# Masked attention scores: row maxima split into three bf16 parts on GpSimd, causal masks only on the diagonal blocks

## The chip, the core and the metric

The kernel runs on one core of one Trainium2 chip. Five engines work side by side, each through its own queue in program order: TensorE (PE, with its weight loads PEld), VectorE (DVE), ScalarE (ACT), GpSimd (POOL) and SyncE (SP, which issues most DMAs). They wait for each other by semaphores. The metric is device time in microseconds: the kernel before took 677.0 us, the median of three runs (675.83 to 677.92).

## The reference, cut to what matters

Two layers, each with a recurrence ("condition"), a causal attention over 4 batches of 256 tokens with 16 heads of 16 dimensions, a second condition and a feed-forward part (a quantised linear layer in the first, a mixture of 32 experts in the second). The change lies in the two attentions:

```
q, k, v = proj(Wq, bq), proj(Wk, bk), proj(Wv, bv)           # 16 heads of 16
scores = einsum('bhsd,bhtd->bhst', q, k) / sqrt(16)
scores = where(t > s, -inf, scores)                          # causal
attn = softmax(scores, axis=-1)
out = einsum('bhst,bhtd->bhsd', attn, v);  y = out @ Wo.T + bo
```

## The kernel before, in words

All engines' programs are written by hand in one function, `build`; the order on an engine is the order of the code, and waits stand where the code has `wait_ge`. Each attention goes through 16 quads v of four heads (batch b = v // 4, place u = v % 4). Four heads of 16 dimensions sit in slots of 32 partitions, so four products with 32 rows each can stand on PE at once. The PSUM tile S holds one bank per head, with 384 columns: query tile 0 against key tile 0, and query tile 1 against both key tiles. The scores of a quad are made twice:

- `scores` (L688, L692): queries on partitions. It starts with a product of the identity and a mask of 384 columns per head and adds q times k. `maxima` (L1095, DVE) reduces them along the keys and writes the negated maxima into `negmax`, one column in 32.
- `neg_mm` (L720): PE turns `negmax` in fp32 by a product with the identity; `neg_out` (L452, ACT) copies the turned rows to SBUF as `neg_rows`.
- `turned_scores` (L702, L706, L710): keys on partitions. A mask again, then k times q, and `pick` (a row of ones per slot) times `neg_rows`, which adds each query's negated maximum to its column. It waits for the maximum of the quad after, since both forms use S.
- `exps` (L445, ACT) takes the exponential of S; `pv` (L739) multiplies by the values and sums the rows.

On PE a step of the loop is: the scores of quad v + 1, `pv` of v - 1, the turned scores of v, `neg_mm` of v + 1, then one of the projections in 11 of 16 steps per layer: queries or keys (L638), values (L664) or the output (L676). The turning of v + 1 thus stands in front of the projection and of the scores of v + 2, which also wait for the exponential of v. On DVE the maximum of v + 1 is followed by a share of the recurrence of another batch: in even steps two small tensor_scalar pieces (L958), a forward and a backward scan (L967, L979) and the scaling of the attention output; in odd steps the two scans of the other half and five products (L998 to L1017 or L1033). In the last step of batches 1 to 3 the residual of the batch before (L1115) comes first. In layer 1 the last two steps have no recurrence.

POOL does little before the experts: fills with zeros and ones, a maximum over partitions of the weight (L342) before the first maximum, one of the activations (L346) between the layers, four additions (L350) before the second attention, and from 389.93 us on the scattering of rows.

Of the kernel before, what the change touches and what calls it, by code (L numbers as in the profile page):

```python
# [13 lines left out]
P = 128  # L14
# [14 lines left out]
SLOT = 32  # L29
# [29 lines left out]
def build(nc, A, out):  # L59
    ctx = ExitStack()  # L60
    with ctx:
        def sb(name, shape, dt=F32):
            return ctx.enter_context(nc.sbuf_tensor(name, shape, dt))
# [31 lines left out]
        causal_b = sb("causal_b", [P, 2, 3 * P], BF16)  # L95
# [15 lines left out]
        negmax = sb("negmax", [P, 2, T // P, HPT, SLOT])  # L111
        neg_rows = sb("neg_rows", [P, 2, T])
        pick = sb("pick", [P, P])
# [210 lines left out]
        def _(eng):  # L324
            eng.memset(v_sb[:, :, :, :, :], 0.0).then_inc(sem("v_zeroed"), 1)
            eng.memset(negmax[:, :, :, :, :], 0.0).then_inc(sem("negmax_zeroed"), 1)
# [4 lines left out]
            for i in range(HPT):  # L331
                eng.memset(pick[i * SLOT:i * SLOT + 1, :], 1.0).then_inc(sem("pick_made"), 1)
            eng.wait_ge(sem("pick_made"), 1 + HPT)
            for par in range(2):
# [5 lines left out]

            eng.wait_ge(sem("amax_w"), 1)
            eng.partition_all_reduce(gmax[:, 1:2], amax_w[:, :], P, bass.bass_isa.ReduceOp.max)\  # L342
               .then_inc(sem("gmax_w"), 1)

# [3 lines left out]
            for b in range(B):  # L348
                eng.wait_ge(sem("y8_made"), b + 1)
                eng.tensor_tensor(x[:, :, tok(b)], x[:, :, tok(b)], y8[:, :, tok(b)], ALU.add).then_inc(sem("x_res_8"), 1)  # L350

# [36 lines left out]
        def _(eng):  # L388
# [58 lines left out]
            def neg_out(L, v):  # L447

                eng.wait_ge(sem(f"neg_mm_{L}"), v + 1)
                if v >= 2:  # L450
                    eng.wait_ge(sem(f"turned_score_{L}"), v - 1)
                eng.activation(neg_rows[:, v % 2, :], TB[:, 0, 0:T], ACT.Copy).then_inc(sem(f"neg_out_{L}"), 1)  # L452
# [180 lines left out]
        def _(eng):  # L633
# [45 lines left out]

            def scores(L, v):  # L680

                b, u = v // QUADS, v % QUADS
                if u == 0:
                    eng.wait_ge(sem(f"k_out_{L}"), b + 1)
                if v >= 2:
                    eng.wait_ge(sem(f"exp_{L}"), v - 1)
                for i in range(HPT):
                    eng.matmul(S[:, i, 0:3 * P], ident_b[:, :], causal_b[:, 0, :], start=True, stop=False)  # L688
                for st, cols in HALVES:
                    for i in range(HPT):  # L690
                        rows = slice(i * SLOT, (i + 1) * SLOT)
                        ins = eng.matmul(S[:, i, cols], q_sb[rows, b % 2, u, st * P:(st + 1) * P],  # L692
                                         k_sb[rows, b % 2, u // 2, 0:P * (st + 1)], start=False, stop=st == 1)
                ins.then_inc(sem(f"score_{L}"), 1)

            def turned_scores(L, v):

                b, u = v // QUADS, v % QUADS
                eng.wait_ge(sem(f"max_{L}"), min(v + 2, B * QUADS))
                eng.wait_ge(sem(f"neg_out_{L}"), v + 1)  # L700
                for i in range(HPT):
                    eng.matmul(S[:, i, 0:3 * P], ident_b[:, :], causal_b[:, 1, :], start=True, stop=False)  # L702
                for kt, (q_cols, cols) in enumerate(((slice(0, T), slice(0, T)), (slice(P, T), slice(T, 3 * P)))):
                    for i in range(HPT):
                        rows = slice(i * SLOT, (i + 1) * SLOT)
                        eng.matmul(S[:, i, cols], k_sb[rows, b % 2, u // 2, kt * P:(kt + 1) * P],  # L706
                                   q_sb[rows, b % 2, u, q_cols], start=False, stop=False)
# [4 lines left out]
                ins.then_inc(sem(f"turned_score_{L}"), 1)  # L712
# [216 lines left out]
        def _(eng):  # L929
# [158 lines left out]
            def maxima(L, v):  # L1088

                eng.wait_ge(sem(f"score_{L}"), v + 1)  # L1090
                eng.wait_ge(sem("negmax_zeroed"), 1)
                if v >= 2:
                    eng.wait_ge(sem(f"neg_mm_{L}"), v - 1)
                for st, cols in HALVES:
                    ins = eng.tensor_reduce(negmax[:, v % 2, st, :, 0], S[:, :, cols], AX.X, ALU.max, negate=True)  # L1095
                ins.then_inc(sem(f"max_{L}"), 1)
# [267 lines left out]
def layout(inputs):  # L1364
# [23 lines left out]
    a["causal"] = np.stack([np.concatenate([m, np.zeros((P, P)), m], 1) for m in (causal, causal.T)], 1).astype(bf16)  # L1388
# [40 lines left out]
```

## Time and profile before

| | |
|---|---|
| three runs | 675.83, 677.92, 677.0 us |
| the profiled execution | 678.75 us, its span 676.9 us |
| mean granted PE clock | 0.925 |
| busy: PE, DVE, ACT, POOL | 523.4, 432.0, 275.4, 211.8 us |
| first and last maximum, layer 0 | 42.19 and 168.54 us |
| first and last maximum, layer 1 | 219.54 and 341.48 us |

Busy time is a sum over stages with different limits, so the attentions have to be read by themselves. A row of the timeline has the start, the busy time and the engine, the line and what is written from what; where an engine stood idle before it, the end of the row says for how long and who ended the wait. A granted clock of 1.00 is the 2.4 GHz level of PE, 0.50 the 1.2 GHz level.

### The profile page before, as it was taken

The numbers are of one execution on the slowest core, as the hardware profiler recorded it, in microseconds if no ns is written. First come the engines' busy times: TensorE is split into PE (matmuls) and PEld (weight loads), VectorE is DVE, ScalarE is ACT, GpSimd is POOL, SyncE is SP. The second block draws the span as 40 slices with busy tenths as digits, with TensorE's granted clock in tenths as the row PEclk, the third lists the DMA queues.
The fourth block names the chain that finished last, engine by engine and source line by source line (L and its number), as shares of the span: only waits on it lengthen the run. The fifth ranks groups of instructions, "written<-read, shape, count | busy, mean of one in ns | idle before, by whom it ended". The sixth has DMA issues, their size and how long they took to land.

```text
span 676.9 us, 12242 instructions
## 1 busy us (share of the span) xinstructions
PE 523.4 (77%) x4564; PEld 407.6 (60%) x4564; DVE 432.0 (64%) x834; ACT 275.4 (41%) x557; POOL 211.8 (31%) x169
## 2 busy tenths in 40 slices
PE   0278799998716779999875689169999999999950
PEld 0156566665404456666654355059999999999940
DVE  3748699999882779999936833036566566566510
ACT  3323464654533445454534111024444444444420
POOL 2000000000012000000000577705778777687772
PEclk9999799999966999999996599679999999999995
DMA  7999910000000000000003233275997869769423
GB/s 279 267 219 223 227 47 1 2 2 1 1 1 0 1 2 1 2 1 2 2 1 135 91 116 110 98 225 143 220 216 197 221 163 228 210 174 225 108 23 68
DMA packets 56716, 71.97 MB, mean 106 GB/s; under 512 B 11777, under 2 KB 45036, under 8 KB 56544
## 3 DMA queue, kind: packets, MB, share of 16 engines
q1 hardware_dynamic: 40272, 57.48, 30.2%
q0 software_dynamic: 16400, 13.87, 11.1%
q8 instruction: 30, 0.49, 0.3%
q14 instruction: 14, 0.11, 0.1%
HBM read 42.22 MB, written 37.04 MB: 117 GB/s over the span
## 4 chain that ended last, share of the span: by engine, by line
PE 49%; DVE 26%; issue 9%; POOL 7%; ACT 5%; DMA 2%; POOLq 0%; SPq 0%; DVEq 0%
PE S L894 14%; DVE negmax L1095 8%; PE PJ L907 8%; POOL xe_rows L358 6%; PE OB L907 4%; PE TB L879 3%; PE S L692 3%; PE S L706 2%; DVE both L979 2%; PE PJ L676 2%; PE S L702 2%; PE PJ L638 2%; DVE fwd L967 2%; PE S L688 2%; PE S L710 2%
## 5 line engine op out<-in xcount | busy, mean ns | idle before, releaser
L894 PE MATMUL S<-xgT,wgu_s 128*128 128x384 f32 x576 | 108.6, 341 | 1.2 <-DVE hidden_f L1336 1.2
L358 POOL DMA_INDIRECT xe_rows<-x_tok,slot_i x48 | 47.2, 984 | 182.5 <-ACT x_tok L577 168.1
L894 PEld LDWEIGHTS S<-xgT,wgu_s 128*128 128x128 f32 x576 | 99.3, 189 | 1.5 <-issue 1.4
L369 POOL DMA_INDIRECT out<-sig,y_token x48 | 75.9, 1581 | 46.6 <-ACT sig L612 33.9
L1095 DVE TENSOR_REDUCE negmax<-S 128x4 f32<-128x512 f32 x64 | 58.3, 952 | 46.0 <-PE S L692 34.1
L369 POOL DMA_INDIRECT odd_out<-sig,y_token x48 | 76.6, 1595 | 24.4 <-ACT sig L612 12.3
L445 ACT ACTIVATE prob<-S 128x1536 f32<-128x1536 f32 x32 | 46.4, 1449 | 66.1 <-PE S L710 66.1
L907 PE MATMUL PJ<-x8m,hidden_f 128*128 128x256 f32 x256 | 60.5, 379 | 1.4 <-ACT sig L612 1.4
L1333 DVE TENSOR_TENSOR hidden_f<-ek,S 128x384 f32<-128x384 f32 x32 | 17.7, 554 | 56.9 <-ACT ek L595 56.9
L907 PEld LDWEIGHTS PJ<-x8m,hidden_f 128*128 128x128 f32 x256 | 47.9, 190 | 6.7 <-issue 1.8
L346 POOL PARTITION_ALL_REDUCE amax_x<-amax_x x1 | 0.4, 380 | 162.2 <-DVE amax_x L1085 162.2
L1325 DVE TENSOR_TENSOR xgT<-TB,xgT 128x384 fp32r<-128x384 f32 x64 | 32.9, 552 | 25.6 <-ACT xgT L602 25.5
L612 ACT ACTIVATE sig<-PJ,y_weight 128x256 f32<-128x256 f32 x64 | 26.8, 471 | 54.1 <-PE OB L907 52.4
L879 PE MATMUL TB<-ident,ratio 128*128 128x128 f32 x192 | 27.6, 282 | 20.2 <-DMA ratio<-xe_rows 19.6
L702 PE MATMUL S<-causal_b,ident_b 128*128 128x384 bf16 x128 | 26.5, 330 | 19.3 <-DVE negmax L1095 19.3
L638 PE MATMUL PJ<-cst,wq 128*128 128x256 f32 x64 | 18.6, 442 | 28.5 <-DVE cst L1033 28.5
L979 DVE TENSOR_TENSOR_SCAN both<-decay_t,fwd 128x512 f32<-128x512 f32 x32 | 39.2, 1225 | 1.1
L595 ACT ACTIVATE ek<-S 128x384 f32<-128x384 f32 x32 | 15.7, 490 | 59.4 <-PE S L894 59.4
L688 PE MATMUL S<-causal_b,ident_b 128*128 128x384 bf16 x128 | 27.4, 339 | 15.3 <-ACT k_sb L489 8.4
L967 DVE TENSOR_TENSOR_SCAN fwd<-decay_t,ek 128x512 f32<-128x512 f32 x32 | 38.9, 1214 | 0.0
L879 PEld LDWEIGHTS TB<-ident,ratio 128*128 128x128 f32 x192 | 23.8, 146 | 24.0 <-DMA ratio<-xe_rows 20.0
L602 ACT ACTIVATE xgT<-TB 128x384 fp32r<-128x384 f32 x64 | 28.4, 504 | 21.5 <-PE TB L879 21.1
(178 smaller groups left out, 1018.0 us busy)
## 6 DMA issues: line engine op xcount, KB each, us to landing
xe_rows<-x8m SPq DMA_DIRECT2D x4, 3468.0 KB, 41.9
ratio<-xe_rows SPq DMA_DIRECT2D x32, 433.5 KB, 4.1
ek<-in_wgu SPq DMA_DIRECT2D x32, 384.0 KB, 4.6
x8m<-in_wd SPq DMA_DIRECT2D x32, 256.0 KB, 2.9
x<-in_x SPq DMA_DIRECT2D x1, 1024.0 KB, 7.3
odd_out<-x8m SPq DMA_DIRECT2D x1, 1024.0 KB, 29.3
out<-side SPq DMA_DIRECT2D x8, 128.0 KB, 5.5
out<-odd_out POOLq DMA_DIRECT2D x1, 1024.0 KB, 7.9
```

The costliest lines, as they stand in the source:

```text
L358: eng.indirect_dma_start(xe_rows, bass.IndirectOffsetOnAxis(slot_i[:, t, k:k + 1], 0), x_tok[:, t, :], None, bounds_check=ROWS - 1, oob_is ...
L369: eng.indirect_dma_start((out, odd_out)[j % 2], bass.IndirectOffsetOnAxis(y_token[:, j, t:t + 1], 0), ye_sb[:, j % 2, t, :], None, bounds_ ...
L445: eng.activation(prob[:, v % 2, :, :], S[:, :, 0:3 * P], ACT.Exp).then_inc(sem(f"exp_{L}"), 1)
L688: eng.matmul(S[:, i, 0:3 * P], ident_b[:, :], causal_b[:, 0, :], start=True, stop=False)
L702: eng.matmul(S[:, i, 0:3 * P], ident_b[:, :], causal_b[:, 1, :], start=True, stop=False)
L879: ins = eng.transpose(TB[:, k, t * P:(t + 1) * P], xg[:, j % RINGE, t, k * P:(k + 1) * P], ident[:, :])
L894: ins = eng.matmul(S[:, m, 0:CAP], fast(wgu_s[:, j % 2, a, k, m * P:(m + 1) * P]), fast(xgT[:, j % 2, b, k, :]), start=n == 0, stop=n == N ...
L907: ins = eng.matmul(dst, hidden_f[:, j % 2, part, t * P:(t + 1) * P], wd[:, j % RINGE, part, :], start=part == 0, stop=part == 1)
L967: eng.tensor_tensor_scan(flat(fwd[:, kv, :, :]), decay_t[:, buf, 0:NC * T], ek_of(kv, b), 0.0, ALU.mult, ALU.add).then_inc(sem("forward"), 1)
L979: eng.tensor_tensor_scan(flat(both[:, kv, :, :])[:, ::-1], decay_t[:, buf, NC * T:0:-1], flat(fwd[:, kv, :, :])[:, ::-1], 0.0, ALU.mult, A ...
L1095: ins = eng.tensor_reduce(negmax[:, v % 2, st, :, 0], S[:, :, cols], AX.X, ALU.max, negate=True)
L1325: eng.tensor_tensor(fast(xgT[:, j % 2, LO, k, :]), TB[:, k, 0:CAP], xgT[:, j % 2, HI, k, :], ALU.subtract)\
```

## The change

POOL splits the fp32 negated maxima of a quad into three bf16 parts (a copy to bf16, the rest, its copy, the rest of that), in four instructions of 128 x 8 elements that each wait for the one before. PE turns the three parts as bf16 columns, three products of 128 columns (query tile 1 stands twice, so that one product per head of 384 columns can add them), and `pick` has three rows of ones per slot. Masks are products of 128 columns, only for the two diagonal blocks of a head, and stand behind the scores. The maxima now wait for POOL's split of two quads ago and no longer for the turning.

```diff
+            def split_maxima(L, v):
+                at = 4 * (B * QUADS * L + v)
+                eng.wait_ge(sem(f"max_{L}"), v + 1)
+                if v >= 2:
+                    eng.wait_ge(sem(f"neg_mm_{L}"), v - 1)
+                settle(eng, "pool")
+                eng.tensor_copy(neg_parts[:, v % 2, :, :, 0], negmax[:, v % 2, :, :]).then_inc(sem("split"), 1)
+                eng.wait_ge(sem("split"), at + 1)
+                eng.tensor_tensor(neg_rest[:, :, :], negmax[:, v % 2, :, :], neg_parts[:, v % 2, :, :, 0], ALU.subtract)\
+                   .then_inc(sem("split"), 1)
+                eng.wait_ge(sem("split"), at + 2)
+                eng.tensor_copy(neg_parts[:, v % 2, :, :, 1], neg_rest[:, :, :]).then_inc(sem("split"), 1)
+                eng.wait_ge(sem("split"), at + 3)
+                eng.tensor_tensor(neg_parts[:, v % 2, :, :, 2], neg_rest[:, :, :], neg_parts[:, v % 2, :, :, 1], ALU.subtract)\
+                   .then_inc(sem("split"), 1)
...
+            def mask_diagonals(turned):
+                for i in range(HPT):
+                    for lo in (0, 2 * P):
+                        ins = eng.matmul(S[:, i, lo:lo + P], ident_b[:, :], causal_b[:, turned, :], start=False,
+                                         stop=lo > 0, skip_group_check=True)
+                return ins
...
-                for i in range(HPT):
-                    eng.matmul(S[:, i, 0:3 * P], ident_b[:, :], causal_b[:, 0, :], start=True, stop=False)
                 for st, cols in HALVES:
...
+                mask_diagonals(0).then_inc(sem(f"score_{L}"), 1)
...
-                    eng.matmul(S[:, i, 0:3 * P], ident_b[:, :], causal_b[:, 1, :], start=True, stop=False)
+                    rows = slice(i * SLOT, (i + 1) * SLOT)
+                    eng.matmul(S[:, i, 0:3 * P], pick[rows, :], neg_rows[rows, v % 2, :], start=True, stop=False,
+                               skip_group_check=True)
...
-                    for i in range(HPT):
-                        rows = slice(i * SLOT, (i + 1) * SLOT)
-                        ins = eng.matmul(S[:, i, cols], pick[rows, :], neg_rows[rows, v % 2, q_cols], start=False,
-                                         stop=kt == 1)
...
+                mask_diagonals(1).then_inc(sem(f"turned_score_{L}"), 1)
...
-                eng.wait_ge(sem(f"max_{L}"), v + 1)
+                eng.wait_ge(sem("split"), 4 * (B * QUADS * L + v + 1))
...
-                for st in range(T // P):
-                    ins = eng.matmul(TB[:, 0, st * P:(st + 1) * P], negmax[:, v % 2, st, :, :].rearrange("p i s -> p (i s)"),
-                                     ident[:, :], start=True, stop=True)
+                for n, st in enumerate((0, 1, 1)):
+                    ins = eng.matmul(TB[:, 0, n * P:(n + 1) * P], neg_parts[:, v % 2, st, :, :].rearrange("p i s -> p (i s)"),
+                                     ident_b[:, :], start=True, stop=True)
```

On PE, the second turned scores of layer 0 and the turning behind them, in the order of the kernel before:

```order
L702 MATMUL S<-causal_b,ident_b 128x384 [waits neg_out_0,max_0]
L702 MATMUL S<-causal_b,ident_b 128x384 x3
L706 MATMUL S<-q_sb,k_sb 128x256 x4
L710 MATMUL S<-neg_rows,pick 128x256 x4
L706 MATMUL S<-q_sb,k_sb 128x128 x4
L710 MATMUL S<-neg_rows,pick 128x128 x4
L720 MATMUL TB<-ident,negmax 128x128 [waits neg_out_0,max_0]
L720 MATMUL TB<-ident,negmax 128x128
```

The same place on PE in the changed kernel, whose line numbers are about 30 higher:

```order
L738 MATMUL S<-neg_rows,pick 128x384 [waits neg_out_0,max_0]
L738 MATMUL S<-neg_rows,pick 128x384 x3
L743 MATMUL S<-q_sb,k_sb 128x256 x4
L743 MATMUL S<-q_sb,k_sb 128x128 x4
L712 MATMUL S<-causal_b,ident_b 128x128 x8
L753 MATMUL TB<-ident_b,neg_parts 128x128 [waits neg_out_0,split]
L753 MATMUL TB<-ident_b,neg_parts 128x128 x2
```

Eight products of picked maxima became four, the masks moved from the front to the back and from four to eight, and the turning waits for `split` in place of the maximum.

```order
L342 ISA
L342 ISA gmax<-amax_w 128x1 [waits amax_w]
L346 ISA amax_x<-amax_x 128x4 [waits amax_x]
L350 ISA
L350 TENSOR_TENSOR x<-x,y 128x2x256 [waits y8_made] x4
```

The same place on POOL in the changed kernel, to the end of the second split:

```order
L362 ISA
L362 ISA gmax<-amax_w 128x1 [waits amax_w]
L351 CAST neg_parts<-negmax 128x8 [waits neg_parts_zeroed,max_0]
L353 ISA
L353 TENSOR_TENSOR neg_rest<-negmax,neg_parts 128x8 [waits split]
L356 CAST neg_parts<-neg_rest 128x8 [waits split]
L358 TENSOR_TENSOR neg_parts<-neg_rest,neg_parts 128x8 [waits split]
L351 CAST neg_parts<-negmax 128x8 [waits max_0]
```

## Rows read from the trace of the kernel before

**Rows 1.** The page's slices of the span, the granted clock of TensorE

```profile
PEclk9999799999966999999996599679999999999995
```

**Rows 2.** Windows of single quads: length, busy time by engine (instructions), granted clock, DMA

```profile
128.47:136.65 8.18, 7.67 (x104) 5.37 (x103) 7.60 (x11) 5.65 (x11) 0.00 (x0) 1.00 0.01 2
136.65:144.83 8.18, 7.67 (x104) 5.37 (x103) 7.24 (x14) 4.61 (x10) 0.00 (x0) 1.00 0.01 2
144.83:153.30 8.47, 7.96 (x108) 5.52 (x107) 8.30 (x12) 3.74 (x7) 0.00 (x0) 1.00 0.01 2
160.85:168.54 7.69, 6.25 (x100) 3.98 (x99) 7.52 (x10) 3.66 (x6) 0.00 (x0) 1.00 0.01 2
```

**Rows 3.** Timeline of one quad with a projection, and what DVE starts in others

```profile
130.21 1.22 DVE L967 TENSOR_TENSOR_SCAN fwd<-decay_t,ek 128x512 f32<-128x512 f32 x1
130.35 0.82 PE L702 MATMUL S<-causal_b,ident_b 128*128 128x384 bf16 x4 [0.51 <-DVE negmax L1095]
131.10 0.71 PE L706 MATMUL S<-q_sb,k_sb 32*128 32x256 f32 x8
131.64 0.61 PE L710 MATMUL S<-neg_rows,pick 32*128 32x256 f32 x8
131.66 1.23 DVE L979 TENSOR_TENSOR_SCAN both<-decay_t,fwd 128x512 f32<-128x512 f32 x1
132.62 0.71 PE L720 MATMUL TB<-ident,negmax 128*128 128x128 f32 x4
132.76 1.45 ACT L445 ACTIVATE prob<-S 128x1536 f32<-128x1536 f32 x1 [1.91 <-PE S L710]
133.17 1.89 PE L638 MATMUL PJ<-cst,wk 128*128 128x256 f32 x8
...
134.90 0.81 PE L688 MATMUL S<-causal_b,ident_b 128*128 128x384 bf16 x4
136.65 1.82 DVE L1095 TENSOR_REDUCE negmax<-S 128x4 f32<-128x512 f32 x2 [0.41 <-PE S L692]
138.39 0.60 DVE L958 TENSOR_SCALAR eu<-side,vec 128x256 f32<-128x256 f32 x2
...
146.57 0.87 DVE L1115 SCALAR_TENSOR_TENSOR x<-PJ,vec,x 128x256 f32<-128x256 f32 x2
```

**Rows 4.** Groups of 90 to 170 us: weight loads of the masks, count, busy, mean ns

```profile
L688 PEld LDWEIGHTS S<-causal_b,ident_b 128*128 128x128 bf16 x40 | 3.7, 98 | 4.7 <-ACT prob L445 2.2
```

**Rows 5.** Timeline of POOL at the start, a fill of one element per partition

```profile
5.60 0.11 POOL L338 MEMSET inner<- 128x1 f32 x1
```

**Rows 6.** Timeline between the two attentions: POOL's additions, DVE and ACT beside them

```profile
198.73 0.69 ACT L561 ACTIVATE y<-S,scale_ab 128x512 bf16<-128x512 f32 x1 [1.86 <-PE S L785]
201.16 2.71 POOL L350 TENSOR_TENSOR x<-x,y 128x512 f32<-128x512 f32 x2 [7.46 <-issue]
204.64 0.69 DVE L1127 TENSOR_TENSOR c_all<-c_all,x8m 128x512 f32<-128x512 f32 x1
204.74 1.61 POOL L350 TENSOR_TENSOR x<-x,y 128x512 f32<-128x512 f32 x1 [0.88 <-ACT y L561]
205.37 1.53 DVE L1129 TENSOR_TENSOR x<-c_all,x8m 128x512 bf16<-128x512 f32 x1
208.78 1.15 POOL L350 TENSOR_TENSOR x<-x,y 128x512 f32<-128x512 f32 x1 [2.44 <-ACT y L561]
```

**Rows 7.** Timeline of the first maxima and scores of layer 0, and of two later ones

```profile
42.19 1.82 DVE L1095 TENSOR_REDUCE negmax<-S 128x4 f32<-128x512 f32 x2 [11.62 <-issue]
44.88 0.81 PE L688 MATMUL S<-causal_b,ident_b 128*128 128x384 bf16 x4
47.09 1.81 DVE L1095 TENSOR_REDUCE negmax<-S 128x4 f32<-128x512 f32 x2
...
74.75 1.46 PE L688 MATMUL S<-causal_b,ident_b 128*128 128x384 bf16 x4 [3.40 <-ACT k_sb L489]
77.87 1.82 DVE L1095 TENSOR_REDUCE negmax<-S 128x4 f32<-128x512 f32 x2 [5.23 <-PE S L692]
```

More of the change, by code:

```diff
@@ L94, in build @@
         ident_b = sb("ident_b", [P, P], BF16)
-        causal_b = sb("causal_b", [P, 2, 3 * P], BF16)
+        causal_b = sb("causal_b", [P, 2, P], BF16)
         decay_qg = sb("decay_qg", [P, CONDS * NC, B])
@@ L110, in build @@
         bq_masked = sb("bq_masked", [P, NC, 2])
-        negmax = sb("negmax", [P, 2, T // P, HPT, SLOT])
-        neg_rows = sb("neg_rows", [P, 2, T])
-        pick = sb("pick", [P, P])
+        negmax = sb("negmax", [P, 2, T // P, HPT])
+        neg_rest = sb("neg_rest", [P, T // P, HPT])
+        neg_parts = sb("neg_parts", [P, 2, T // P, HPT, SLOT], BF16)
+        neg_rows = sb("neg_rows", [P, 2, 3 * P], BF16)
+        pick = sb("pick", [P, P], BF16)
         ones_p = sb("ones_p", [P, 2, SLOT])
@@ L325, in _ @@
             eng.memset(v_sb[:, :, :, :, :], 0.0).then_inc(sem("v_zeroed"), 1)
-            eng.memset(negmax[:, :, :, :, :], 0.0).then_inc(sem("negmax_zeroed"), 1)
+            eng.memset(neg_parts[:, :, :, :, :], 0.0).then_inc(sem("neg_parts_zeroed"), 1)
             eng.memset(pick[:, :], 0.0).then_inc(sem("pick_made"), 1)
@@ L331, in _ @@
             for i in range(HPT):
-                eng.memset(pick[i * SLOT:i * SLOT + 1, :], 1.0).then_inc(sem("pick_made"), 1)
+                eng.memset(pick[i * SLOT:i * SLOT + 3, :], 1.0).then_inc(sem("pick_made"), 1)
             eng.wait_ge(sem("pick_made"), 1 + HPT)
@@ L343, in _ @@
                .then_inc(sem("gmax_w"), 1)
+            eng.wait_ge(sem("neg_parts_zeroed"), 1)
+            for v in range(B * QUADS):
+                split_maxima(0, v)
             eng.wait_ge(sem("amax_x"), B)
@@ L350, in _ @@
                 eng.tensor_tensor(x[:, :, tok(b)], x[:, :, tok(b)], y8[:, :, tok(b)], ALU.add).then_inc(sem("x_res_8"), 1)
+            for v in range(B * QUADS):
+                split_maxima(1, v)
             eng.wait_ge(sem("slots_zeroed"), 80)
@@ L451, in neg_out @@
                     eng.wait_ge(sem(f"turned_score_{L}"), v - 1)
-                eng.activation(neg_rows[:, v % 2, :], TB[:, 0, 0:T], ACT.Copy).then_inc(sem(f"neg_out_{L}"), 1)
+                eng.activation(neg_rows[:, v % 2, :], TB[:, 0, 0:3 * P], ACT.Copy).then_inc(sem(f"neg_out_{L}"), 1)
             def totals_inverse(L, b, c):
@@ L691, in scores @@
                         rows = slice(i * SLOT, (i + 1) * SLOT)
-                        ins = eng.matmul(S[:, i, cols], q_sb[rows, b % 2, u, st * P:(st + 1) * P],
-                                         k_sb[rows, b % 2, u // 2, 0:P * (st + 1)], start=False, stop=st == 1)
-                ins.then_inc(sem(f"score_{L}"), 1)
+                        eng.matmul(S[:, i, cols], q_sb[rows, b % 2, u, st * P:(st + 1) * P],
+                                   k_sb[rows, b % 2, u // 2, 0:P * (st + 1)], start=st == 0, stop=False,
+                                   skip_group_check=True)
+                mask_diagonals(0).then_inc(sem(f"score_{L}"), 1)
             def turned_scores(L, v):
@@ L701, in turned_scores @@
                 for i in range(HPT):
[L702 removed]
+                    rows = slice(i * SLOT, (i + 1) * SLOT)
+                    eng.matmul(S[:, i, 0:3 * P], pick[rows, :], neg_rows[rows, v % 2, :], start=True, stop=False,
+                               skip_group_check=True)
                 for kt, (q_cols, cols) in enumerate(((slice(0, T), slice(0, T)), (slice(P, T), slice(T, 3 * P)))):
@@ L706, in turned_scores @@
                         eng.matmul(S[:, i, cols], k_sb[rows, b % 2, u // 2, kt * P:(kt + 1) * P],
-                                   q_sb[rows, b % 2, u, q_cols], start=False, stop=False)
-                    for i in range(HPT):
-                        rows = slice(i * SLOT, (i + 1) * SLOT)
-                        ins = eng.matmul(S[:, i, cols], pick[rows, :], neg_rows[rows, v % 2, q_cols], start=False,
-                                         stop=kt == 1)
-                ins.then_inc(sem(f"turned_score_{L}"), 1)
+                                   q_sb[rows, b % 2, u, q_cols], start=False, stop=False, skip_group_check=True)
+                mask_diagonals(1).then_inc(sem(f"turned_score_{L}"), 1)
             def neg_mm(L, v):
-                eng.wait_ge(sem(f"max_{L}"), v + 1)
+                eng.wait_ge(sem("split"), 4 * (B * QUADS * L + v + 1))
                 if v:
                     eng.wait_ge(sem(f"neg_out_{L}"), v)
-                for st in range(T // P):
-                    ins = eng.matmul(TB[:, 0, st * P:(st + 1) * P], negmax[:, v % 2, st, :, :].rearrange("p i s -> p (i s)"),
-                                     ident[:, :], start=True, stop=True)
+                for n, st in enumerate((0, 1, 1)):
+                    ins = eng.matmul(TB[:, 0, n * P:(n + 1) * P], neg_parts[:, v % 2, st, :, :].rearrange("p i s -> p (i s)"),
+                                     ident_b[:, :], start=True, stop=True)
                 ins.then_inc(sem(f"neg_mm_{L}"), 1)
@@ L1090, in maxima @@
                 eng.wait_ge(sem(f"score_{L}"), v + 1)
-                eng.wait_ge(sem("negmax_zeroed"), 1)
                 if v >= 2:
-                    eng.wait_ge(sem(f"neg_mm_{L}"), v - 1)
+                    eng.wait_ge(sem("split"), 4 * (B * QUADS * L + v - 1))
                 for st, cols in HALVES:
-                    ins = eng.tensor_reduce(negmax[:, v % 2, st, :, 0], S[:, :, cols], AX.X, ALU.max, negate=True)
+                    ins = eng.tensor_reduce(negmax[:, v % 2, st, :], S[:, :, cols], AX.X, ALU.max, negate=True)
                 ins.then_inc(sem(f"max_{L}"), 1)
@@ L1387, in layout @@
     causal = np.where(np.arange(P)[None, :] > np.arange(P)[:, None], -1e30, 0.0)
-    a["causal"] = np.stack([np.concatenate([m, np.zeros((P, P)), m], 1) for m in (causal, causal.T)], 1).astype(bf16)
+    a["causal"] = np.stack([causal, causal.T], 1).astype(bf16)
     proj = f32["L1_attn_w_project"]
```

## The prediction

> **What bounds the kernel now.** I read the slices of the page for the stages, then the windows of single quads, then the timeline of one quad. The change touches only the two attentions. There the work goes in quads of four heads, 16 per layer, and one quad lasts from one maximum on VectorE (DVE) to the next: 8.18 us where TensorE (PE) has a projection behind the turned scores, 8.47 us where DVE also adds a residual, 7.69 us without a projection [rows 2]. In the first kind PE is busy for 7.67 us and DVE for 7.60 us: both are nearly full, so whichever is lengthened sets the quad, and a cut on one engine gains little more than the idle time of the other.
>
> The order inside a quad [rows 3] (the maximum that starts at 128.47 takes 1.82 and ends at 130.29): PE starts the turned scores at 130.35; the turning of the negated maxima at 132.62; the projection at 133.17; the next scores at 134.90; their maximum starts at 136.65. ScalarE's exponential runs from 132.76 beside the turning and the projection. The two waits that decide are thus PE's for the maximum, and DVE's for the scores.
>
> **PE's part.** Turned scores take 2.27 us (130.35 to 132.62): masks 0.75 us for four of 384 columns, so 0.19 each; then fp32 scores and picks, the first four of 256 columns 0.54 us (131.10 to 131.64). After: a bf16 column costs 0.19/384 = 0.49 ns, an fp32 one 1.7 (the projection's four products of 256 columns take 1.73 us). Four bf16 picks of 384 columns, side by side on four groups of rows like the fp32 ones: 0.54 x 1.5 x 0.49/1.7 = 0.23 us (0.75 if one after the other). The fp32 scores stay, 0.54 + 0.27 us. Eight masks of 128 columns: by columns 0.19/3 = 0.063 each, by the weight load 0.098 each [rows 4], so 0.5 to 0.8 us; I take 0.65. Sum 1.7 us (1.5 to 2.4), 0.6 saved. The masks of the plain scores go from 0.75 to the same 0.65, so scores to maximum stays at 1.75 us (134.90 to 136.65). The turning goes from 0.55 us (132.62 to 133.17) to three single passes, 0.3; with the projection 2.0 instead of 2.28 us. ScalarE's copy of 384 instead of 256 columns is wanted only behind the next maximum: nothing.
>
> **What is put in its place.** The turning used to start on the maximum itself; now it waits for four GpSimd (POOL) instructions, each waiting for the one before. Behind it on PE's queue stand the projection and the next scores. A POOL instruction on few elements takes 0.11 us [rows 5]; with a semaphore I count 0.25, so an undisturbed chain ends 1.0 us after the maximum, before the 1.7 of the turned scores: hidden. But DVE works on without a pause behind the maximum, and POOL and DVE hold each other up [rows 6]: POOL's add at 204.74 started 0.10 us behind a DVE product of 0.69 and took 1.61 us, against 1.15 for the one at 208.78 with DVE idle; the DVE instruction of the same size at 205.37 then took 1.53 us, 0.84 more than the product. Each waits for the other's whole instruction. The DVE product has two operands in SBUF, and so has a scan; no row shows a scan against POOL, so its price lies between nothing and its full 1.22 us. I take the full one, since the nearest row is that product.
>
> The Trainium skill ("SBUF — State Buffer", section "SBUF: two separate sides") says that the two engines lock a shared port pair for a whole instruction, a DVE one with two SBUF inputs counting against a POOL one that reads SBUF. The waits at 204.74 and 205.37 agree; by it a scan blocks too, as I assume.
>
> *Odd quads* (after the maximum a scan of 1.22, a small piece in the 0.23 before 131.66, a scan of 1.23, then products of 0.69 [rows 3, 6]). Times from the maximum's end: the first POOL copy waits for the scan until 1.15, ends 1.3; the difference slips in behind the small piece, 1.45 to 1.6; the second copy waits for the second scan, 2.8 to 2.9; the last difference for a product, ends 3.65. Turning at 3.7, projection and it 2.0, scores 1.75, maximum 1.82: 9.3 us, +1.1. If POOL loses one more turn, 4.9 and +2.3.
> *Even quads* (two pieces of 0.30 first, as at 138.39 [rows 3], then the scans): the chain ends at 2.4 if both gaps are caught and at 3.65 if one is missed; I take 3.0: 8.6 us, +0.45 (0 to +1.9).
> *With a residual*: its 0.87 us, as at 146.57 [rows 3], reads PSUM and one SBUF operand; the chain passes inside. DVE is the bound at 8.47 and loses 2 x 0.15 to POOL: +0.3.
> *Without a projection*: the turning's wait lies beside the exponential (1.45); the next scores start at 3.7 + 0.4 = 4.1 us, as today (7.69 less 1.75 and 1.82). DVE adds 0.3 of port time to 7.52 of busy in 7.69 [rows 2]: +0.15.
> Per layer three odd, five even (four in layer 1, whose last pair has no scans), two residual, the rest without effect of a projection: 6 x 1.1 + 9 x 0.45 + 4 x 0.3 + 13 x 0.15 = 13.8 us. Ends: -8 (no scan blocks, rival 1) and +34 (each chain loses a turn more, 6 x 2.3 + 9 x 1.9 + 3.2).
>
 PE's queue has the first turning before the second scores, and the first maximum ends at 44.0: 44.1 + 7.4 + three steps of 0.25 + 0.3 = 52.6 us for the second scores, now 44.88 [rows 7]; +7.7, less 0.5 that the second maximum (47.09) waits for DVE today. PE stands still meanwhile; after such a stop the scores at 74.75 ran at the granted 0.50, the 1.2 GHz level, and took 3.12 us to the maximum instead of 1.75 [rows 7] (the 7 in the fifth slice [rows 1]): +1.4. Sum +8.6 (1.2 to 13: DMA is busy then and the load may be slower). A second load, before the next use of the old library, starts behind layer 0's last split, a few us after the maximum of 168.54, and is wanted at 193.7 (201.16 less 7.46): nothing.
>
> The Trainium skill ("GPSIMD Engine Reference", section "2.1 Instruction dispatch") gives about 6 us for the first call to a freshly loaded kernel. The gap here, 7.46 us, is near; by the page's figure, as an estimate, the total would be 1.4 us less.
>
> **Sum.** The profiled execution is 678.75 us (span 676.9), 1.75 above the median of 677.0. 678.75 + 13.8 + 8.6 = 701.2 us; on the median 699.4, so I forecast 699. Its own range: from rival 3's 686 to 677 + 34 + 8.6 = 720.
>
> **Rivals.**
> 1. *The port wait does not bite*, because scans leave POOL alone: the chain is hidden at 1.0. Then quads fall to what DVE needs, odd 7.6 + 0.3 (-0.3), even 7.24 + 0.3 (-0.65), residual 8.5 (0) by the busy times [rows 2]: -6 x 0.3 - 9 x 0.65 = -7.7; where POOL takes no port time either, -0.6, -0.9: -11.7. For: no row shows a scan blocked. Against: [rows 6]. With the load: 677 - 7.7 + 8.6 = 678 to 674 us; with a load that costs its lower end, 667. It decides from a chain that ends before 1.7. This is the rival on the faster side.
> 2. *POOL starves and PE falls to the low clock*: with waits of 3 us in a quad, each stop of PE may bring 0.50 as in slice five, 1.4 us a time; ten such on top of the forecast's upper half give 677 + 24 + 9 + 14 = 724. Against: the quad at 160.85 leaves PE idle for 1.4 of its 7.69 us and keeps 1.00 [rows 2].
> 3. *The load alone costs*: the chain is late, but by no more than PE saves in a quad: 677 + 8.6 = 686, the forecast's lower end.
>
> **Chances.** Forecast (686 to 720, rival 3 in it) 0.70; rival 1 0.22, of which faster 0.15, same 0.05, slower 0.02; rival 2 0.08. What a measurement here can tell is 0.3%, 2 us. Faster 0.15, same 0.05, slower 0.80. Range: 674 to 722, leaving out some 0.08 below and 0.08 above.
>
> **What the profile would show.** Right: turning on PE ended by POOL, starting 2.4 to 4 us after the maximum; POOL instructions of over 1 us beside scans; about 8 us of idle PE and POOL before the second scores; quads of 9.3 us with a projection in odd places, 8.5 to 8.8 with a residual; DVE no longer full. Wrong: POOL's four done within 1.7 us, or PE's turning idle ended by something other than POOL; a first difference within 2 us of the first copy; turned scores above 2.3 us, which would add 0.6 per quad of PE time for another reason.

## The result and the profile after

The changed kernel takes 699.56 us, the median of four runs (696.89 to 699.99), against 677.46 us for the kernel before: a ratio of 1.030 with a 95% interval of 1.026 to 1.034. The forecast was 699. Its profiled execution took 699.62 us with a span of 697.7, so 20.8 us of span have to be found. The starts of the maxima in the two timelines place them:

| stretch | before | after | difference |
|---|---|---|---|
| start to the first maximum | 42.19 | 40.94 | -1.25 |
| first to second maximum | 4.90 | 13.91 | +9.01 |
| second to last maximum, layer 0 (14 quads) | 121.45 | 129.08 | +7.63 |
| to the first maximum of layer 1 | 51.00 | 52.26 | +1.26 |
| first to last maximum, layer 1 (15 quads) | 121.94 | 128.39 | +6.45 |
| last maximum to the end | 335.4 | 333.1 | -2.3 |

The first two maxima and the quads behind them make up 23.1 us. The other three stretches together give back 2.3 us. They are not laid to the change: the start of the first maximum alone lies between 38.40 and 42.19 us in the traces of this case.

The page's slices of the kernel after answer to [rows 1]. In slices 6 to 10, within the attention of layer 0, the granted clock now falls to 8 twice, in the seventh and the ninth; before, it stood at 9 in all of them. The fourth, behind the first split, is at 5.

```profile
PEclk9985998989985889999999589859999999999995
```

The first split, selected rows of POOL, PE and DVE in the timeline (start, busy time, engine, line, what is written from what, and in brackets the idle time before it and who ended it; beside [rows 7]):

```profile
40.94 1.82 DVE L1127 TENSOR_REDUCE negmax<-S 128x4 f32<-128x512 f32 x2 [11.19 <-PE S L712]
...
42.93 0.22 POOL L351 CAST neg_parts<-negmax 128x8 bf16<-128x8 f32 x1 [12.66 <-issue]
...
50.89 0.20 POOL L353 TENSOR_TENSOR neg_rest<-negmax,neg_parts 128x8 f32<-128x8 f32 x1 [7.75 <-issue]
...
51.46 0.23 POOL L358 TENSOR_TENSOR neg_parts<-neg_rest,neg_parts 128x8 bf16<-128x8 f32 x1
51.75 0.50 PE L753 MATMUL TB<-ident_b,neg_parts 128*128 128x128 bf16 x3 [8.27 <-POOL neg_parts L358]
52.18 1.67 PE L726 MATMUL S<-k_sb,q_sb 32*128 32x128 f32 x16
```

Between the first copy and the first difference POOL waits 7.75 us for nothing that the profile shows, and PE stands still behind it for 8.27. Behind that gap the operations start 0.27 and 0.30 us after each other: this is what they cost by themselves.

Then the quads, as windows (length, busy time of PE, PEld, DVE, ACT, POOL with instructions, granted clock, DMA), beside [rows 2]:

```profile
102.30:112.62 10.32, 8.13 (x99) 5.87 (x102) 8.35 (x11) 5.32 (x11) 2.84 (x4) 0.83 0.01 2
122.85:131.32 8.47, 7.30 (x115) 5.19 (x118) 8.30 (x12) 3.61 (x7) 1.82 (x4) 1.00 0.01 2
131.32:139.94 8.62, 5.75 (x83) 4.14 (x79) 7.36 (x14) 4.93 (x9) 2.75 (x4) 1.00 0.01 3
```

From the fifth quad of a layer on there are three kinds with a projection: 8.62 to 8.72 us, 8.47 or 8.35 with a residual as before, and five quads of 10.2 to 10.3 us whose mean granted clock is 0.83. The last two quads of a layer, without a projection, take 7.35 and 7.69. The timeline of the last window shown, selected rows of PE, POOL and DVE, shows the first loss (beside [rows 3]):

```profile
131.32 1.81 DVE L1127 TENSOR_REDUCE negmax<-S 128x4 f32<-128x512 f32 x2
...
133.20 0.34 PE L738 MATMUL S<-neg_rows,pick 32*128 32x384 bf16 x4 [1.25 <-DVE negmax L1127]
133.33 0.22 POOL L351 CAST neg_parts<-negmax 128x8 bf16<-128x8 f32 x1 [6.42 <-DVE negmax L1127]
...
133.62 1.20 DVE L1000 TENSOR_TENSOR_SCAN fwd<-decay_t,ek 128x512 f32<-128x512 f32 x1
133.63 1.19 POOL L353 TENSOR_TENSOR neg_rest<-negmax,neg_parts 128x8 f32<-128x8 f32 x1
134.12 0.62 PE L712 MATMUL S<-causal_b,ident_b 128*128 128x128 bf16 x8
...
134.88 0.22 POOL L356 CAST neg_parts<-neg_rest 128x8 bf16<-128x8 f32 x1
135.05 1.22 DVE L1012 TENSOR_TENSOR_SCAN both<-decay_t,fwd 128x512 f32<-128x512 f32 x1
135.18 1.12 POOL L358 TENSOR_TENSOR neg_parts<-neg_rest,neg_parts 128x8 bf16<-128x8 f32 x1
...
136.36 0.34 PE L753 MATMUL TB<-ident_b,neg_parts 128*128 128x128 bf16 x3 [1.62 <-POOL neg_parts L358]
136.54 1.95 PE L667 MATMUL PJ<-cst,wq 128*128 128x256 f32 x8
```

The first window, selected rows of POOL, PE and DVE from the end of its maximum on, shows the second:

```profile
104.04 1.21 DVE L1000 TENSOR_TENSOR_SCAN fwd<-decay_t,ek 128x512 f32<-128x512 f32 x1
...
104.31 0.95 POOL L351 CAST neg_parts<-negmax 128x8 bf16<-128x8 f32 x1 [5.65 <-DVE negmax L1127]
...
105.35 0.20 POOL L353 TENSOR_TENSOR neg_rest<-negmax,neg_parts 128x8 f32<-128x8 f32 x1
105.49 1.22 DVE L1012 TENSOR_TENSOR_SCAN both<-decay_t,fwd 128x512 f32<-128x512 f32 x1
105.61 1.11 POOL L356 CAST neg_parts<-neg_rest 128x8 bf16<-128x8 f32 x1
106.81 0.58 POOL L358 TENSOR_TENSOR neg_parts<-neg_rest,neg_parts 128x8 bf16<-128x8 f32 x1
...
107.44 0.50 PE L753 MATMUL TB<-ident_b,neg_parts 128*128 128x128 bf16 x3 [1.71 <-POOL neg_parts L358]
...
107.73 3.43 PE L667 MATMUL PJ<-cst,wk 128*128 128x256 f32 x8
...
111.09 0.94 PE L726 MATMUL S<-k_sb,q_sb 32*128 32x128 f32 x16
```

In both, two or three of POOL's four operations last until a DVE instruction ends (1.19 beside the scan of 1.20; the copies at 104.31 and 105.61 end within 0.02 us of the scans), and PE has nothing to do for 1.6 to 1.7 us. In the second, the turning and the projection behind that wait then ran at a mean granted clock of 0.55 (107.40 to 111.10 us), mostly at the 1.2 GHz level, and the projection took 3.43 us instead of 1.95.

### The profile page after: what moved, and what is told of

It reads as the page before. It is cut to its first block, busy times and chain, and to the rows that moved or that the text cites. A ratio compares the mean times of both kernels' runs of the same rounds, so it can differ in the third digit from the quotient of the medians.

```text
span 697.7 us, 12083 instructions
## 1 busy us (share of the span) xinstructions
PE 502.9 (72%) x4404; PEld 397.7 (57%) x4404; DVE 432.5 (62%) x834; ACT 279.3 (40%) x557; POOL 291.0 (42%) x297
## 4 chain that ended last, share of the span: by engine, by line
PE 42%; DVE 26%; POOL 13%; issue 11%; ACT 4%; DMA 2%; POOLq 0%; SPq 0%; DVEq 0%
PE S L927 14%; DVE negmax L1127 8%; PE PJ L940 7%; POOL xe_rows L387 6%; PE OB L940 4%; PE PJ L667 3%; PE S L726 3%; PE TB L912 3%; PE PJ L705 3%; DVE both L1012 2%; DVE fwd L1000 2%; PE S L712 2%; POOL neg_parts L358 2%; POOL neg_rest L353 2%; POOL neg_parts L356 1%
## 5 line engine op out<-in xcount | busy, mean ns | idle before, releaser
L351 POOL CAST neg_parts<-negmax 128x8 bf16<-128x8 f32 x32 | 14.3, 447 | 205.6 <-DVE negmax L1127 193.0
L753 PE MATMUL TB<-ident_b,neg_parts 128*128 128x128 bf16 x96 | 12.2, 243 | 48.9 <-POOL neg_parts L358 48.9
L712 PE MATMUL S<-causal_b,ident_b 128*128 128x128 bf16 x512 | 43.1, 232 | 0.0
L712 PEld LDWEIGHTS S<-causal_b,ident_b 128*128 128x128 bf16 x512 | 31.3, 103 | 16.4 <-issue 12.8
L726 PE MATMUL S<-k_sb,q_sb 32*128 32x256 f32 (+1 forms) x512 | 33.8, 383 | 9.4 <-ACT k_sb L518 8.1
```

The costliest lines, as they stand in the source:

```text
L712: ins = eng.matmul(S[:, i, lo:lo + P], ident_b[:, :], causal_b[:, turned, :], start=False, stop=lo > 0, skip_group_check=True)
```

## The experiments

The theory at this point: the loss is (a) a code load in front of the first two-input operation, paid on the path; (b) two waits of POOL for DVE's shared port in each chain, longer than the turned scores cover; (c) the low clock that PE falls to behind its wait for POOL, in some quads. The main rival: the bf16 form itself on PE and ACT, or a GpSimd that is slow whatever DVE does. Ratios are to the kernel before on the same chip, with their 95% intervals.

**e1, the load moved.**

```diff
+            eng.wait_ge(sem("ones_p_made"), 3)
+            eng.tensor_tensor(warm[:, :], ones_p[:, 0, 0:8], ones_p[:, 1, 0:8], ALU.subtract).then_inc(sem("warmed"), 1)
             eng.wait_ge(sem("neg_parts_zeroed"), 1)
```

> One small subtraction on GpSimd is added right behind the maximum over the weights, long before the first maxima; all else is as in the changed kernel (699.6). Theory (the 7.75-us idle before the first two-input operation is code being loaded, and it is paid once, on the path): the idle moves to the new subtraction, where nothing waits, the first split takes about 1.4 us, the second maximum comes about 5 us after the first instead of 13.9, and the kernel takes 689 to 693, some 7 to 9 us less. Rival (the idle belongs to the first split itself, or the start is set by something else that was late): 698 to 700, with 12 to 14 us still between the first two maxima.

Measured: 686.58 us (682.66 to 688.88), ratio 1.016 [1.010, 1.021]. The idle went to the added instruction:

```profile
37.40 0.20 POOL L366 TENSOR_TENSOR warm<-ones_p 128x8 f32<-128x8 f32 x1 [7.28 <-issue]
41.58 0.22 POOL L352 CAST neg_parts<-negmax 128x8 bf16<-128x8 f32 x1 [3.98 <-issue]
41.88 0.38 POOL L354 TENSOR_TENSOR neg_rest<-negmax,neg_parts 128x8 f32<-128x8 f32 x1
```

The first two maxima are 6.61 us apart instead of 13.91. The load is on the path and costs 7.3 us. The total fell by more, 13 us, which my theory had not said: in this profile (682.66 us, the fastest of the runs) no quad from the fifth of a layer on is longer than 8.73, so there the low clock of (c) stayed away too. Its four runs scatter over 6 us, which suggests that this differs from one execution to the next; only this one has a profile. That clean profile is used below as the one with warm quads.

**e2, one POOL operation instead of four**: the lines from the first difference on are dropped, and the counts of `split` go from 4 to 1.

> GpSimd makes only the first of the three bf16 parts, one copy in place of four operations; the other two parts stay zero, so the maxima that are subtracted are rounded to bf16. TensorE, the evictions and the masks are as in the changed kernel. Theory (the loss is the chain of GpSimd's four operations, the code load before the first two-input one, and the low clock that the waits bring): no load, a turning that waits for GpSimd 0.3 to 1.2 us after the maximum instead of 3.3, quads of 8.4 to 8.6 us everywhere, and 672 to 680, some 20 to 27 us less than the changed kernel. Rival (the loss is in the bf16 form on TensorE and ScalarE, the wider eviction, or in putting GpSimd in between at all): 688 or more.

Measured: 669.93 us (665.51 to 673.70), 0.989 [0.986, 0.992], 30 us less than the changed kernel and a little below the forecast band. The rival falls: POOL between DVE and PE costs nothing as long as it is one copy (e5 below, without POOL, takes 670.18). The low clock is not gone in e2: behind the first few quads five even ones still took 8.43 or 8.44 us, with projections of 2.44 to 2.71.

**e4, the masks alone**, on the kernel before:

```diff
-                for i in range(HPT):
-                    eng.matmul(S[:, i, 0:3 * P], ident_b[:, :], causal_b[:, 0, :], start=True, stop=False)
...
+                mask_diagonals(0).then_inc(sem(f"score_{L}"), 1)
...
+                mask_diagonals(1).then_inc(sem(f"turned_score_{L}"), 1)
```

> The kernel before, with the one part alone that puts the masks on the diagonal blocks only and adds them last, in both kinds of scores; the maxima go their old way, in fp32 and past GpSimd. Theory (this part is cheap and off the path, since VectorE bounds most quads): 673 to 678, no change or up to 3 us less. Rival (masks added last hold up the maxima, because eight more small matmuls stand between the last scores and the maximum): 682 to 690, with 0.3 to 0.6 us more in every quad.

Measured: 669.46 us (668.07 to 672.06), 0.990 [0.987, 0.993]: a gain of 7.3 us, more than either side expected. The windows of two quads that lasted 8.18 us before (DVE's maximum used to wait 0.8 and 0.4 us for PE at their ends):

```profile
99.00:106.71 7.71, 6.39 (x96) 4.95 (x92) 7.25 (x15) 4.09 (x8) 0.00 (x0) 1.00 0.01 2
122.88:130.59 7.71, 7.23 (x112) 5.53 (x115) 7.54 (x10) 5.98 (x12) 0.00 (x0) 1.00 0.01 2
```

**e5, the maxima in bf16 straight from DVE**, no POOL:

```diff
-                    ins = eng.tensor_reduce(negmax[:, v % 2, st, :], S[:, :, cols], AX.X, ALU.max, negate=True)
+                    ins = eng.tensor_reduce(neg_parts[:, v % 2, st, :, 0], S[:, :, cols], AX.X, ALU.max, negate=True)
```

> The changed kernel without GpSimd's split: VectorE writes the negative maxima as bf16 straight into the first part, the other two parts stay zero (the maxima that are subtracted are rounded to bf16, which the division by the sums takes out again). Theory (GpSimd's part is all of the loss, and what remains of the change gains a little): 668 to 676, below the kernel before, no quad at 10 us, and the turning waits for the maximum alone. Rival (TensorE's and ScalarE's part of the change costs time too): 680 or more.

Measured: 670.18 us (667.68 to 673.36), 0.990 [0.987, 0.994]. As forecast in time, but not in form: with POOL gone some even quads take 7.33 us and others 8.45, where the masks alone take 7.71 throughout. The longer ones have a granted clock of 0.80:

```profile
99.29:107.74 8.45, 6.57 (x67) 5.14 (x71) 7.24 (x14) 4.75 (x9) 0.00 (x0) 0.80 0.00 0
132.36:139.69 7.33, 5.90 (x87) 4.28 (x83) 7.16 (x14) 3.82 (x7) 0.00 (x0) 1.00 0.00 0
```

In the first of them PE had waited for DVE in front of the turned scores, and the projection behind took 2.87 us (rows of PE in the timeline):

```profile
101.17 0.34 PE L715 MATMUL S<-neg_rows,pick 32*128 32x384 bf16 x4 [2.20 <-DVE neg_parts L1105]
...
103.41 2.87 PE L682 MATMUL PJ<-o_sb,wo 128*128 128x256 f32 x8
```

So PE loses its clock behind a wait for DVE too; POOL is not what does it.

**e3, DVE holds still** (e1, and DVE waits for the split after each maximum):

```diff
                 ins.then_inc(sem(f"max_{L}"), 1)
+                eng.wait_ge(sem("split"), 4 * (B * QUADS * L + v + 1))
```

> As the run with the early subtraction (e1, 686.6), and VectorE goes on after each maximum only when GpSimd's four operations are done. Theory (each of the four is short, and two of them are held until one of VectorE's scans or its two-pass scalar operation ends): beside a still VectorE every operation lasts 0.2 to 0.4 us, the four take 1.2 to 1.7 us from the maximum's end, TensorE's turning waits for GpSimd less than 0.3 us behind the turned scores, and VectorE pays 1.2 to 1.7 us in each of 32 quads: 690 to 712. Rival (the operations are slow by themselves, or by what TensorE and ScalarE do): two of the four still take over 0.9 us, the four take 3 us or more, and the kernel takes 720 or more.

Measured: 712.83 us (711.55 to 713.24), 1.052 [1.048, 1.056]. The time is a shade over the upper end; the groups decide. POOL's four operations in the changed kernel (count, busy time, mean ns, idle before):

```profile
L358 POOL TENSOR_TENSOR neg_parts<-neg_rest,neg_parts 128x8 bf16<-128x8 f32 x32 | 24.2, 756 | 2.6
L353 POOL TENSOR_TENSOR neg_rest<-negmax,neg_parts 128x8 f32<-128x8 f32 x32 | 21.6, 675 | 10.3 <-issue 7.7
L356 POOL CAST neg_parts<-neg_rest 128x8 bf16<-128x8 f32 x32 | 19.4, 606 | 2.1
L351 POOL CAST neg_parts<-negmax 128x8 bf16<-128x8 f32 x32 | 14.3, 447 | 205.6 <-DVE negmax L1127 193.0 <-issue 12.7
```

and beside a DVE that waits:

```profile
L359 POOL TENSOR_TENSOR neg_parts<-neg_rest,neg_parts 128x8 bf16<-128x8 f32 x32 | 7.4, 232 | 2.6
L352 POOL CAST neg_parts<-negmax 128x8 bf16<-128x8 f32 x32 | 7.0, 218 | 265.4 <-DVE negmax L1130 260.3 <-issue 5.1
L357 POOL CAST neg_parts<-neg_rest 128x8 bf16<-128x8 f32 x32 | 7.0, 217 | 2.1
L354 POOL TENSOR_TENSOR neg_rest<-negmax,neg_parts 128x8 f32<-128x8 f32 x32 | 6.6, 205 | 2.6
```

PE and ACT worked as before beside them, so it is DVE alone that stretches them from 0.2 to 0.4-0.8 us. Four operations beside a still DVE are also no loss for PE: except behind the first maximum of each layer its turning does not wait for POOL in this run. One quad, whose maximum ends at 129.71:

```profile
130.77 0.23 POOL L359 TENSOR_TENSOR neg_parts<-neg_rest,neg_parts 128x8 bf16<-128x8 f32 x1
...
131.15 0.33 PE L756 MATMUL TB<-ident_b,neg_parts 128*128 128x128 bf16 x3
```

The Trainium skill ("SBUF — State Buffer", section "SBUF: two separate sides") says that a DVE instruction with two SBUF inputs, against a GpSimd one that reads SBUF, holds the shared port pair for all its length; the scans do (1.19 beside 1.20), and the copies with one SBUF input on POOL wait as the differences do (0.95 and 1.11 above). Not every DVE instruction does so: beside the residual (DVE busy from 124.59 on for 0.86 us, with one input in PSUM and one in SBUF) POOL's copy and difference at 124.86 and 125.16 took 0.22 and 0.20 us.

**e6, PE kept busy** while POOL is awaited:

```diff
+                    for n in range(16):
+                        eng.matmul(TB[:, 0, 3 * P:4 * P], ident_b[:, :], causal_b[:, 0, :], start=True, stop=True)
+                eng.wait_ge(sem("split"), 4 * (B * QUADS * L + v + 1))
```

> The changed kernel, with 16 matmuls of 128 columns into unused columns ahead of TensorE's wait for GpSimd, about 0.9 us of work in place of idling; the code load stays on the path. Theory (the quads of 10.2 us are those in which TensorE fell to its low clock behind that wait, so that the projection took 3.4 us instead of 1.95): the projections stay at 1.95 us, the five quads come down to 8.6 to 8.7, and the kernel takes 688 to 694, some 6 to 11 us less than 699.6. Rival (those quads are long for another reason, and the clock only follows): 697 to 702, quads of 10.2 us still there.

Measured: 690.54 us (687.63 to 691.29), 1.018 [1.014, 1.023]: 9.0 us less with the same load and the same split, and no projection over 1.95 us from the fifth quad of a layer on. The rows of one:

```profile
111.57 1.06 PE L752 MATMUL TB<-causal_b,ident_b 128*128 128x128 bf16 x16
113.36 0.34 PE L755 MATMUL TB<-ident_b,neg_parts 128*128 128x128 bf16 x3 [0.73 <-POOL neg_parts L358]
113.53 1.95 PE L705 MATMUL PJ<-o_sb,wo 128*128 128x256 f32 x8
```

The turning starts hardly earlier than in the changed kernel (3.23 us after the maximum's end here, 3.32 in the quad at 102.30); what follows is faster. The clock was the cause of the five long quads, not a companion.

**e8, e1 and e6 together.**

> The early subtraction and the 16 filler matmuls together. Theory (code load and low clock are two separate terms of the loss that add up): 679 to 685, that is 7 to 9 us below the run with the filler alone and no quad over 9 us with a warm projection in all of them; what is then left over 669.5 (the masks alone) is the split itself, 10 to 14 us, some 0.4 us in each quad that has a projection. Rival (the early subtraction already gave the low clock back, and the filler only adds work): 686 to 690.

Measured: 681.76 us (678.18 to 684.35), 1.0065 [1.0035, 1.0094]: with the stop filled (e6) moving the load gives 8.8 us. So the filler's 9.0 and the load's 8.8 add up. The 13 us of e1 alone were more than the load, since part of the low clock had gone with it.

**e7, e5 with 24 such products in front of the turned scores:**

```diff
-                eng.wait_ge(sem(f"max_{L}"), min(v + 2, B * QUADS))
                 eng.wait_ge(sem(f"neg_out_{L}"), v + 1)
+                for n in range(24):
+                    eng.matmul(TB[:, 0, 3 * P:4 * P], ident_b[:, :], causal_b[:, 0, :], start=True, stop=True)
+                eng.wait_ge(sem(f"max_{L}"), min(v + 2, B * QUADS))
```

> VectorE writes the maxima as bf16 straight into the first part as in the run without GpSimd (e5, 670.2; the other two parts stay zero), and 24 matmuls of 128 columns into unused columns stand ahead of TensorE's wait for the next maximum, in front of the turned scores. Theory (there the quads of 8.45 us are those in which TensorE, now with less work, idles over 2 us for VectorE and falls to the low clock; at the full clock the same quads take 7.33, bound by VectorE): no projection over 2 us, every even quad 7.3 to 7.4, and 659 to 666. Rival (the filler delays the turned scores or the clock falls all the same): 669 to 674.

Measured: 666.32 us (664.46 to 668.66), 0.985 [0.981, 0.989]. No projection of the quads is over 2 us, and the even quads behind the first few take 7.32 to 7.38. The median lies 0.3 us above the theory's band and 3.9 below e5. In e5's profile five quads at the low clock were 1.1 us longer each.

**e10, two parts instead of three**: e1 with the fillers of e7, and the second POOL operation writing bf16.

```diff
-                eng.tensor_tensor(neg_rest[:, :, :], negmax[:, v % 2, :, :], neg_parts[:, v % 2, :, :, 0], ALU.subtract)\
+                eng.tensor_tensor(neg_parts[:, v % 2, :, :, 1], negmax[:, v % 2, :, :], neg_parts[:, v % 2, :, :, 0], ALU.subtract)\
                    .then_inc(sem("split"), 1)
```

> The early subtraction (e1) with a split into two bf16 parts instead of three: GpSimd makes one copy and one subtraction, written as bf16, in place of four operations (the third part stays zero); the 24 fillers stand ahead of the turned scores as in e7 (666.3), which differs from this run by GpSimd's two operations and the early subtraction alone. Theory (TensorE has 1.55 us of turned scores to do after a maximum, and only what GpSimd needs beyond that is lost: one wait for VectorE's port is hidden, the second one is not): the split is done 1.2 to 1.7 us after the maximum's end, the turning waits for GpSimd less than 0.3 us, quads as in e7 within 0.2 us, and 665 to 671. Rival (each GpSimd operation behind the maximum costs its own time on the path): about half of the 15.5 us between e7 and e8 stay, 672 to 677, and the quads with a projection are 0.3 to 0.7 us longer than in e7.

Measured: 667.79 us (666.68 to 668.37), 0.986 [0.982, 0.989]. This is where (b) shows most plainly:

```profile
100.12 0.22 POOL L352 CAST neg_parts<-negmax 128x8 bf16<-128x8 f32 x1 [7.29 <-DVE negmax L1127]
100.42 1.22 POOL L354 TENSOR_TENSOR neg_parts<-negmax,neg_parts 128x8 bf16<-128x8 f32 x1
100.91 0.62 PE L710 MATMUL S<-causal_b,ident_b 128*128 128x128 bf16 x8
101.69 0.34 PE L753 MATMUL TB<-ident_b,neg_parts 128*128 128x128 bf16 x3 [0.16 <-POOL neg_parts L354]
```

The difference still waits out a whole scan (1.22 us), but it ends with the turned scores, and PE waits 0.16 us. A chain of two costs 1.5 us against e7, which is within the scatter of the two; a chain of four costs 15.4 (e8, whose 16 fillers stand behind the turned scores). The cost lies in the second wait for DVE and not in the number of operations, for in e3 four operations without such a wait were done before PE needed them.

**e9, e4 with the 24 fillers of e7.**

> The masks alone (e4, 669.5; fp32 maxima, no GpSimd) with the same 24 fillers ahead of the turned scores. In e4 the projections of the quads ran at 1.89 us already. Theory (a filler gives back only what the low clock took): 665 to 670, at most 4 us less, from the first two quads of a layer, and the even quads stay at 7.7. Rival (fillers shorten a quad in another way too): under 664, even quads of 7.5 or less.

Measured: 685.25 us (683.99 to 686.31), 1.013 [1.009, 1.016], 16 us slower than e4. Both expectations missed. PE is full in every quad that has a projection, from the fifth on; two of them:

```profile
100.26:108.87 8.61, 8.61 (x136) 6.88 (x140) 7.26 (x14) 4.86 (x10) 0.00 (x0) 1.00 0.01 2
108.87:117.48 8.61, 8.61 (x136) 6.88 (x139) 8.39 (x12) 3.48 (x7) 0.00 (x0) 1.00 0.01 2
```

The sum could have been made beforehand: in e4 two such quads (99.00 to 115.18) hold 6.39 and 7.99 us of PE, 7.2 on the mean, and 24 fillers add 1.45, so 8.64. In e7, whose turnings and picks are bf16, the same fillers bring PE to 8.55 and 6.96 us in a pair of quads, which just fits. A filler is free only up to the idle time.

## Why the prediction was right, and where only its sum was

**The first split** was priced at +8.6 and cost +9.01. The load was taken as about 7.4 us from [rows 6]; it was 7.75, and e1 gets 7.3 back by moving it. The second scores were put at 52.6 us and started at 52.18. The low clock behind the stop was put at 1.4 us: e8 has 1.14 less than e1 between the two maxima (5.47 against 6.61). The Trainium skill ("GPSIMD Engine Reference", section "2.1 Instruction dispatch") gives about 6 us for such a load; the gaps seen here are all longer: 7.75, 7.28 (e1) and 7.52 (e8) at the first two-input operation, 7.44 before the additions between the layers, and 6.79 to 8.14 over all the traces. The second load, between the layers, was hidden as forecast: the maximum over partitions at 209.94 us waited for DVE.

**The mechanism in the quads was right.** The chain ended 3.17 us after the maximum's end in the quad at 131.32 (3.0 forecast, within 2.4 to 3.65) and 3.27 in the one at 102.30 (3.65); PE's turning waited for POOL, POOL's operations lasted over 1 us beside scans. Rival 1, in which a scan leaves POOL alone, falls with these rows and with e3. Turned scores took 1.54 us (133.20 to 134.74; 1.7 forecast) and eight masks 0.62 (0.65).

**The quads' sum of +13.8 came out at +14.08, but of other parts.** Quad by quad, with the warm values from e1:

| quads | forecast | warm, e1 against before | after against e1, low clock in five quads |
|---|---|---|---|
| odd with projection, 6 | 6.6 | 1.3 | 3.1 (two quads) |
| even with projection | 4.05 (9) | 3.6 (8, each 0.44 to 0.46) | 4.9 (three quads) |
| residual, 4 | 1.2 | 0 | 0 |
| the rest | 1.95 | 2.1 | below 0, -0.9 |

- *The odd term failed*, by 5.3 us. Its +1.1 took 8.18 us, the one odd quad of [rows 2], as the length before; four of the six odd quads lasted 8.55 to 9.05, three of them because DVE and not PE bounded them. And 9.3 was too long by 0.57: the chain's last difference waited 0.58 us for what was left of a DVE instruction instead of a full product (0.38 us), and scores to maximum took 1.53 us (111.09 to 112.62), where I had left them at 1.75 although the masks were now small (0.22).
- *DVE's loss to POOL was sized at 2 x 0.15 us a quad and is nothing*: residual quads keep 8.47, and DVE's busy time went from 432.0 to 432.5 us in all. POOL's difference at 105.35 falls between two scans, and the second scan starts 0.24 us behind the end of the first, against 0.23 before [rows 3].
- *The low clock belonged to rival 2, at 0.08, and supplied 8.0 us of the measured 14.1.* Five quads grew by 1.55 to 1.68 us each; I had 1.4 a time for ten of them. What I held against it, the quad at 160.85 that idles 1.4 us at full clock [rows 2], was no bound. How long PE stops does not decide alone: the quad at 131.32 stopped for 1.62 us and kept its clock, while three of the five long quads stopped for the same 1.62. With the stop filled, e6 gives 9.0 us back.

So the forecast of 699 was met by a sum in which terms were too large by about as much as another was missing: 5.3 us for the odd quads and 1.2 for the residual ones, against 8.0 for the clock. The likeliest case (686 to 720) had two of the causes right, the load and the chain's waits, and left out the third; its half microsecond of agreement is luck.

**What I did not see is the gain inside the change.** The masks alone are worth 7.3 us (e4). The prediction gave the masks 0.1 us in each form of the scores and let it vanish under the chain. In e4's quad at 99.00 the turned scores took 1.98 us (2.27 before) and scores to maximum 1.53 (1.75 before); together 0.5, which is what an even quad lost that PE had bounded (8.18 to 7.71). The changed kernel loses about 22 us on the kernel before, or 30 on the one with its masks alone (e4). The runs one below the other divide these 30: some 9 for the clock (e6), 9 for the load (e8 against e6), and 15 for the chain of four (e8 against e7), less 3 that the bf16 form gives (e7 against e4; these two differ in the fillers too). In the profiles 13 of the 15 lie in the quads from the fifth of a layer on.

**The two fastest versions beat both kernels and are within 1.5 us of each other** (e2, e4 and e5 beat both too, at 669.5 to 670.2): e7 at 666.3 us, with the maxima rounded to bf16 on the way out of DVE, and e10 at 667.8, with two bf16 parts. What stays open is why some quads lose the clock behind a stop of 1.6 us and others keep it, and so probably why executions of e1 differ.

## What to carry to other kernels

Before handing a small step to GpSimd, look at what VectorE does just then: each of a chain's operations can wait out a scan or a product of VectorE, and only as many waits are free as the consumer has other work for (here one, 1.54 us of turned scores). Where a GpSimd operation brings a code load, as the first two-input one did here behind a maximum over partitions (7.75 us), put one of its kind early, off the path, where the load is seen by nobody. And price a new wait on TensorE twice: its length, and the slower matmuls behind it; a filler wins that back only if the sum of TensorE's work still fits the quad.

## What the runs showed of the hardware

- A one-input copy on GpSimd (fp32 to bf16, 128 x 8) is held by VectorE's scans like a two-input difference: 0.22 us beside an idle VectorE, 0.95 to 1.11 beside a scan, and 0.22 again beside the residual's instruction with one SBUF input.
- For operations this small the cost fell on one side: VectorE's busy time was 0.5 us longer with 128 of them than without, but GpSimd spent 79.5 us on work that takes 28.0 when VectorE waits. An addition of 128 x 512 did hold VectorE, for 0.84 us [rows 6].
- TensorE fell to the 1.2 GHz level behind stops of 1.62 to 2.20 us in some quads (changed kernel, e5) and kept 2.4 GHz behind stops of 1.62 to 1.72 in others (changed kernel, e1); with matmuls into unused columns in the same place (e6, e7, e8) no projection from the fifth quad on fell.
